# A decoder's first self-attention: the bias band added by TensorE, side work at later tiles, larger gathers, and value jobs of the cross-attentions at other key tiles

## The reference, cut to what matters

```python
# first self-attention: 16 heads of 16, on _layernorm(x)
rel = pos[:, None] - pos[None, :]                       # query minus key
bias = jnp.minimum(rel * slopes[:, None, None], 8.0)    # slopes[h] = 2 ** (-(h + 1) / 2)
scores = einsum('bhqd,bhkd->bhqk', q, k) * D ** -0.5 + bias
x = x + softmax(scores) @ v @ out_proj_weight.T + out_proj_bias
# cross-attention: 8 heads (masked, layer 0) or 16 heads (layer 1) of 64
x = x + (softmax(q @ k.T * 64 ** -0.5) @ v) @ W_o + b_o
```

## Time and profile before

| what | us |
|---|---|
| median of 3 runs (3207.7 to 3210.42) | 3209.64 |
| the profiled execution's own time | 3209.26 |
| its span, first to last instruction | 3207.5 |
| first self-attention, stage start to first score tile | 117.5 to 172.2 |
| its loop, first to last exponential | 173.3 to 509.1 |
| first cross-attention, exponentials | 572.4 to 1317.3 |
| second cross-attention, exponentials | 1564.4 to 3055.0 |

### The profile page before, as it was taken

How to read it: one execution, slowest core, us unless ns; L and a number is a source line. 1 busy time by engine, 2 the same in 40 slices (tenths; PEclk the granted TensorE clock), 3 DMA queues, 4 the chain that set the end, 5 groups by cost and what they waited for, 6 DMA issues and landing times. The chain is left out here.

```text
span 3207.5 us, 38273 instructions
## 1 busy us (share of the span) xinstructions
PE 2823.4 (88%) x12634; PEld 1744.4 (54%) x12634; DVE 1851.7 (58%) x3753; ACT 1302.5 (41%) x2326; POOL 1648.4 (51%) x1404
## 2 busy tenths in 40 slices
PE   6578786899999999688899999999999999999979
PEld 5333344556565565354655655565556556566457
DVE  2356675566666666536555655555565565565556
ACT  1134554444444454311444444444444444444410
POOL 0344402566566666610466665666666666666710
PEclk8778998999999999898899999999999999999979
DMA  8666513232232322100332232232322233222110
GB/s 266 157 167 151 142 15 90 54 99 67 63 89 64 90 58 56 35 0 22 102 73 49 64 101 49 68 73 58 90 66 67 55 99 75 49 67 63 31 53 27
DMA packets 113532, 245.81 MB, mean 77 GB/s; under 512 B 15366, under 2 KB 61703, under 8 KB 112184
## 3 DMA queue, kind: packets, MB, share of 16 engines
q1 hardware_dynamic: 107128, 219.82, 27.6%
q0 software_dynamic: 5696, 23.42, 2.7%
q10 hardware_dynamic: 512, 0.13, 0.0%
HBM read 107.31 MB, written 31.76 MB: 43 GB/s over the span
## 5 line engine op out<-in xcount | busy, mean ns | idle before, releaser
L1009 POOL TENSOR_TENSOR ACC<-ACC,PR 128x512 f32<-128x512 f32 (+1 forms) x1056 | 1331.1, 1283 | 486.2 <-ACT PR L1234 476.8
L1234 ACT ACTIVATE PR<-banks 128x512 f32<-128x512 f32 (+1 forms) x832 | 469.1, 597 | 682.6 <-PE banks L1123 681.2
L1295 DVE TENSOR_REDUCE mx<-banks 128x2 f32<-128x800 f32 (+1 forms) x512 | 504.2, 986 | 406.8 <-PE banks L1075 405.6
L1139 PE MATMUL banks<-PR,V 128*64 128x512 f32 (+1 forms) x2496 | 602.5, 607 | 0.0
L1122 PE MATMUL banks<-QA,KA 128*128 128x512 f32 (+1 forms) x1248 | 535.4, 429 | 9.7 <-DMA QB<-ROW 8.7
L1075 PE MATMUL banks<-KH,QZ 128*128 128x400 f32 (+1 forms) x1536 | 482.7, 372 | 58.2 <-DVE mx L1295 37.9
L1123 PE MATMUL banks<-QB,KB 65*128 65x512 f32 (+1 forms) x1248 | 495.0, 397 | 0.0
L1075 PEld LDWEIGHTS banks<-KH,QZ 128*128 128x128 f32 x1536 | 268.3, 189 | 246.5 <-issue 113.6
L1234 ACT ACTIVATE PR<-banks,small 128x512 f32<-128x512 f32 (+1 forms) x416 | 269.3, 687 | 306.5 <-PE banks L1123 298.8
L1292 DVE CUSTOM_DVE_ANT_0 banks<-banks,maskadd 128x400 f32<-128x400 f32 (+1 forms) x512 | 289.9, 588 | 158.5 <-PE banks L1075 153.0
L1263 DVE TENSOR_TENSOR KB<-banks,KH 64x400 fp32r<-64x400 f32 (+1 forms) x384 | 219.4, 571 | 261.4 <-ACT KH L1167 255.9
(11 more groups left out here) (240 smaller groups left out, 3047.0 us busy)
## 6 DMA issues: line engine op xcount, KB each, us to landing
KA<-KH SPq DMA_DIRECT2D x192, 400.5 KB, 6.7
CX<-ctx_split SPq DMA_DIRECT2D x8, 2403.0 KB, 10.7
WK<-wk_split SPq DMA_DIRECT2D x48, 256.0 KB, 5.7
WV<-wv_split SPq DMA_DIRECT2D x24, 512.0 KB, 3.6
QA<-QZ SPq DMA_DIRECT2D x96, 128.0 KB, 2.3
QB<-QZ SPq DMA_DIRECT2D x96, 128.0 KB, 2.4
first<-in_w_in SPq DMA_DIRECT2D x8, 1024.0 KB, 6.0
second<-in_w_out1T SPq DMA_DIRECT2D x8, 1024.0 KB, 8.7
```

Source lines behind the costliest of these rows:

```text
L1009: pool.tensor_tensor(acc, other, PR[0:r, n % RING, :], ALU.add).then_inc(summed, 1)
L1139: last = pe.matmul(OB[h * DH:(h + 1) * DH, :], V[0:r, g % 4, s, h * DH:(h + 1) * DH], PR[0:r, (n + h) % RING, :], start=(s == 0), stop=(s ...
L1234: act.activation(PR[0:r, n % RING, :], SB[n % 3][0:r, :], ACT.Exp, bias=keybias[0:r, g // pairs, t:t + 1] if masked else 0.0).then_inc(pro ...
L1295: dve.tensor_reduce(mx[:, :, t, c], couples[i % 2 if g == 0 else 0][:, :, 0:w], AX.X, ALU.max).then_inc(mx_done, 1)
```

## The change

- **Band.** TensorE adds it: after the score matmul of a banded tile a second one, fp32, with minus the identity (`minus`, 128 x 128) as weights and the band (128 partitions by up to 128 columns) as moving side accumulates into the same bank. VectorE's subtraction and the semaphore `biased` are gone.
- **Side work.** `LEAD` is 24. The jobs stand at other tiles (p 0, 4, 20, 29; v 45, 48; a 13, 16; o 32, 36; turn 7, row 10, of a batch or a group). ScalarE does a job one tile later than TensorE and HI two tiles later; VectorE does LO four tiles later, v and o two later, and `normalise` at tile 9.
- **Gathers.** `parts` holds three blocks per side, so SyncE stores high twice (HI as soon as it is there), 48 stores of 256 KB in place of 32, and gathers with four DMAs per half of 48 partitions by 8 KB, q before k, 32 DMAs in place of 96. The weights are permuted on the host so that a partition's four rows are adjacent.
- **Start.** TensorE runs `before()` ahead of the wait for the rows, with the two "v" between the second and third "p". GpSimd starts to split only when the first row has landed.
- **Cross-attentions.** Three "v" jobs stand at t 5, 7, 9, four at 4, 5, 7, 9. Mask steps stand at t 11 (step 0), 12 (1 and 2) and 13 (3).

```diff
--- before.py
+++ after.py
@@ -89,7 +89,7 @@
-        self.parts = nc.dram_tensor("parts", (2, 2, 4, P, S), F32).ap()
+        self.parts = nc.dram_tensor("parts", (2, 4, 2, 3, DH, S), F32).ap()
...
@@ -401,10 +401,10 @@
-        LEAD, RING = 22, 8
+        LEAD, RING = 24, 8
...
-        HALF = 12 * 16
+        HALF = 4 * 16
...
@@ -416,25 +416,21 @@
-            return [("p", 0, i) for i in range(4)] + [("v", 0, 0), ("v", 0, 1)]
+            return [("p", 0, 0), ("p", 0, 1), ("v", 0, 0), ("v", 0, 1), ("p", 0, 2), ("p", 0, 3)]
...
-                jobs += {1: [("p", b + 1, 0)], 3: [("p", b + 1, 1)], 17: [("p", b + 1, 2)], 19: [("p", b + 1, 3)],
-                         34: [("v", b + 1, 0)], 37: [("v", b + 1, 1)]}.get(l, [])
+                jobs += {0: [("p", b + 1, 0)], 4: [("p", b + 1, 1)], 20: [("p", b + 1, 2)], 29: [("p", b + 1, 3)],
+                         45: [("v", b + 1, 0)], 48: [("v", b + 1, 1)]}.get(l, [])
...
-                jobs += {13: [("a", b - 1, 0)], 15: [("a", b - 1, 1)], 25: [("o", b - 1, 0)], 29: [("o", b - 1, 1)]}.get(l, [])
-            if n % GN == 6 and n >= GN:
+                jobs += {13: [("a", b - 1, 0)], 16: [("a", b - 1, 1)], 32: [("o", b - 1, 0)], 36: [("o", b - 1, 1)]}.get(l, [])
+            if n % GN == 7 and n >= GN:
...
-            if n % GN == 11 and n // GN + 1 < NG:
+            if n % GN == 10 and n // GN + 1 < NG:
...
@@ -460,6 +456,7 @@
+            minus = sb("minus", [P, P])
...
@@ -491,24 +488,24 @@
-                            for side in range(2):
+                            for side, kinds in ((0, "hlh"), (1, "hhl")):
...
-                                c = 2 * side + half
-                                sp.wait_ge(lo_ready, i + 1)
+                                to = self.parts[b % 2, 2 * side + half]
...
-                                sp.dma_start(self.parts[b % 2, 0, c], raw(HI[:, i % 2, :])).then_inc(hl_out[i % 2], 16)
-                                sp.dma_start(self.parts[b % 2, 1, c], raw(LO[:, i % 2, :])).then_inc(hl_out[i % 2], 16)
-                            for side in range(2):
-                                sp.wait_ge(hl_out[side], 32 * (2 * b + half + 1))
+                                sp.wait_ge(hi_ready, i + 1)
+                                for blk in range(3):
+                                    if kinds[blk] == "h":
+                                        sp.dma_start(to[:, blk], raw(HI[:, i % 2, :])).then_inc(hl_out[i % 2], 16)
+                                sp.wait_ge(lo_ready, i + 1)
+                                sp.dma_start(to[:, kinds.index("l")], raw(LO[:, i % 2, :])).then_inc(hl_out[i % 2], 16)
...
-                            for side, to, parts in ((1, KS, (0, 0, 1)), (0, QS, (0, 1, 0))):
-                                for blk, part in enumerate(parts):
-                                    src = self.parts[b % 2, part, 2 * side + half].rearrange("(i two d) n -> two d i n", two=2, d=D)
-                                    for par in range(2):
-                                        o = DH * par + D * blk
-                                        sp.dma_start(raw(to[o:o + D, b % 2, 4 * half:4 * half + 4, :]), src[par]).then_inc(stacked[half], 16)
+                            for side, to in ((0, QS), (1, KS)):
+                                sp.wait_ge(hl_out[side], 48 * (2 * b + half + 1))
+                                for par in range(2):
+                                    src = self.parts[b % 2, 2 * side + half, par].rearrange("k (d i) n -> (k d) i n", d=D)
+                                    sp.dma_start(raw(to[DH * par:DH * par + 48, b % 2, 4 * half:4 * half + 4, :]), src).then_inc(stacked[half], 16)
...
@@ -519,6 +516,7 @@
+                    pool.wait_ge(row_in, 32)
...
@@ -601,10 +599,11 @@
+                    for x in before():
+                        job(x)
+                    pe.wait_ge(scaled, 1)
...
-                    for x in before():
-                        job(x)
...
@@ -614,8 +613,13 @@
-                        pe.matmul(SB[n % 3][:, :], operand(KS, h, ROWS)[:, t * P:(t + 1) * P], operand(QS, h, ROWS),
-                                  start=True, stop=True).then_inc(sc_ready, 1)
+                        last = pe.matmul(SB[n % 3][:, :], operand(KS, h, ROWS)[:, t * P:(t + 1) * P], operand(QS, h, ROWS),
+                                         start=True, stop=not banded(n))
+                        if banded(n):
+                            o = t * P + int(CLAMP[h % H])
+                            w = min(P, S - o)
+                            last = pe.matmul(SB[n % 3][:, o:o + w], minus[:, :], self.band[:, h % H, 0:w], start=False, stop=True)
+                        last.then_inc(sc_ready, 1)
...
@@ -636,11 +640,9 @@
-                                act.wait_ge(hl_out[j % 2], 32 * (j // 2))
+                                act.wait_ge(hl_out[j % 2], 48 * (j // 2))
...
-                            act.wait_ge(job_done, i + 1)
-                            act.activation(HI[:, j % 2, :], FULL[:, j % 2, :], ACT.Copy).then_inc(hi_ready, 1)
...
@@ -655,26 +657,33 @@
+                    def rounded(x):
+                        j = 4 * x[1] + x[2]
+                        act.wait_ge(job_done, place[x] + 1)
+                        act.activation(HI[:, j % 2, :], FULL[:, j % 2, :], ACT.Copy).then_inc(hi_ready, 1)
+
...
-                    act.wait_ge(scaled, 2)
+                    act.wait_ge(scaled, 3)
...
+                        if x[0] == "p":
+                            rounded(x)
...
-                        if banded(n):
-                            act.wait_ge(biased, bands[n + 1])
-                        else:
-                            act.wait_ge(sc_ready, n + 1)
+                        act.wait_ge(sc_ready, n + 1)
...
-                        for x in at(n):
+                        for x in at(n - 2) if n >= 2 else []:
+                            if x[0] == "p":
+                                rounded(x)
+                        for x in at(n - 1) if n >= 1 else []:
...
@@ -730,6 +739,7 @@
+                    dve.tensor_scalar(minus[:, :], ident[:, :], -1.0, None, ALU.mult).then_inc(scaled, 1)
...
@@ -738,17 +748,15 @@
-                        if banded(n):
-                            o = t * P + int(CLAMP[h % H])
-                            w = min(P, S - o)
-                            dve.wait_ge(sc_ready, n + 1)
-                            s = SB[n % 3][:, o:o + w]
-                            dve.tensor_tensor(s, s, self.band[:, h % H, 0:w], ALU.subtract).then_inc(biased, 1)
-                        for x in at(n):
-                            job(x)
...
-                        if n % GN == 7 and g >= 1:
+                        for x in at(n - 4) if n >= 4 else []:
+                            if x[0] == "p":
+                                job(x)
+                        for x in at(n - 2) if n >= 2 else []:
+                            if x[0] in "vo":
+                                job(x)
+                        if n % GN == 9 and g >= 1:
...
@@ -813,8 +821,10 @@
-            if t >= 4:
-                jobs += values_at(g)[t - 4:t - 3]
+            todo = values_at(g)
+            for x, tile in zip(todo, {0: (), 3: (5, 7, 9), 4: (4, 5, 7, 9), 7: range(4, 11)}[len(todo)]):
+                if tile == t:
+                    jobs.append(x)
...
@@ -1376,8 +1386,9 @@
-                            if masked and g % pairs == 1 and g // pairs + 1 < B and t in (0, 11, 12, 13):
-                                mask_step(g // pairs + 1, (0, 11, 12, 13).index(t))
+                            if masked and g % pairs == 1 and g // pairs + 1 < B:
+                                for c in {11: (0,), 12: (1, 2), 13: (3,)}.get(t, ()):
+                                    mask_step(g // pairs + 1, c)
...
@@ -1852,14 +1863,20 @@
+    def paired(w):
+
+        w = w.copy()
+        w[..., 0:2 * C] = w[..., 0:2 * C].reshape(-1, 4, H // 4, 2, D).transpose(0, 1, 3, 4, 2).reshape(w[..., 0:2 * C].shape)
+        return w
+
...
-        "w0_in": g["L0_attn_in_proj_weight"].T, "b0_in": g["L0_attn_in_proj_bias"],
-        "b0_cols": g["L0_attn_in_proj_bias"][0:2 * C].reshape(4, P).T,
+        "w0_in": paired(g["L0_attn_in_proj_weight"].T), "b0_in": g["L0_attn_in_proj_bias"],
+        "b0_cols": paired(g["L0_attn_in_proj_bias"])[0:2 * C].reshape(4, P).T,
```

More of the change, by code:

```diff
@@ L417, in banded @@
             return S - 1 - t * P > CLAMP[h % H]
-        bands = [0]
-        for n in range(N):
-            bands.append(bands[-1] + banded(n))
         def before():
-            return [("p", 0, i) for i in range(4)] + [("v", 0, 0), ("v", 0, 1)]
+            return [("p", 0, 0), ("p", 0, 1), ("v", 0, 0), ("v", 0, 1), ("p", 0, 2), ("p", 0, 3)]
         def at(n):
@@ L476, in self_attention @@
                 scaled, ones_made, x_based = sem("s_scaled"), sem("s_ones"), sem("s_based")
-                sc_ready, biased, probs, used, mx_ready, mx_done = (
```

(5 more changed lines are left out.)

## The result

The changed kernel takes **3286.5 us** (median of 4 runs, 3275.6 to 3289.8) against 3208.7 of the kernel before: ratio 1.0243, 95% interval 1.0218 to 1.0269. That is 78 us slower where 62 us faster was forecast, and outside the range. The profiled execution took 3285.4 us, its span is 3283.6.

What follows compares the result with a forecast made beforehand. No engine fills the self-attention loop, a ring of short waits; TensorE bounds the cross-attentions, though not every tile. Start -12, loop -21, mask steps -14 and value jobs -15 sum to -62 against 3209.3: 3147 us, range 3110 to 3188.

Steps and rivals of the forecast that it cites:

- The loop: Self-attention loop, 335.8 us before: sum of opposite terms for projections, band, turn, normalise and row's DMA, -21 us.
- Normalise at 9 with row at 10: Self-attention loop: TensorE stands at row behind normalise, 1.5 us in each of 15 groups, +23, ends 0 and +30.
- Band on TensorE: Self-attention loop: 0.35 us per band, 53 us of TensorE, half hidden in its 61 idle us, +27, ends +0 and +75.
- Rival C: Banded loop groups: TensorE becomes the bound through the second matmul, kernel slower by 20 us, 3229; chance 0.04.
- the drain at a change of tiling mode: Banded loop tiles: two mode changes each might drain TensorE; neither proved nor excluded, counted as Rival C's mechanism.
- Projections: Loop groups with "p" jobs: LO four tiles later removes 85% of VectorE's 32.7 us wait for HI, -28.
- Turn one tile later: Self-attention loop: removes about half of TensorE's 25.6 us wait for the copied outputs before "turn", -13.
- The start: Before the loop: earlier first copy, and q gathers sent sooner in fewer, larger DMAs, -12 us.
- SyncE's queue issues 64 fewer gathers and 16 more stores and was idle anyway: The start: the changed counts of gathers and stores on SyncE's queue were taken to cost nothing.
- GpSimd's last piece: GpSimd's splitting starts later; its last piece moves from 385.7 to about 415 to 425, at no cost.
- Mask steps and value jobs: Cross-attentions: later mask steps give -14 us, value jobs moved to odd key tiles give -15 us.

Runs made afterwards that it cites:

- g1: f7 with the next tile's score repeated six times, as overwritten matmuls, before each row job: 3180.0 us.
- f7: f3 with turn, normalise and row moved to tiles 7, 9 and 10, and the two o jobs at 28 and 31: 3223.0 us.
- h1: The whole changed kernel with split stores, plus six overwritten score matmuls before each row job: 3219.5 us.
- e3: The changed kernel with each store issued as two DMAs of 64 partitions (split stores): 3261.5 us.
- g5: f3 with row at tile 10 in place of 11, normalise still at 7, and LEAD 24 in place of 22: 3170.1 us.
- e1: The kernel before with only the band moved to TensorE: 3207.4 us, ratio 1.0010.
- g2: f7 with the band back on VectorE: 3177.9 us.
- h4: g5 with the band back on VectorE: 3175.3 us.
- h3: The whole changed kernel with split stores and the band back on VectorE: 3206.3 us.
- f6: The changed kernel with split stores, ScalarE and VectorE doing each job's result in the tile that issues it (no lags): 3240.0 us.
- e4: The kernel before with only the cross-attention parts, the moved mask steps and value jobs: 3176.4 us, ratio 0.9901.
- f3: The changed kernel with split stores, but the self-attention's side work, lags and LEAD 22 as in the kernel before: 3174.8 us.

## Why the prediction was wrong

- **The loop, -21 forecast, +93 measured. The step that failed is "Normalise at 9 with row at 10", +23 with ends of 0 and +30.** Its mechanism and its own size were right: TensorE stands at row 13 times, 19.4 us in all. What it left out is what an idle TensorE does next: its clock falls to 1.2 GHz, and that is worth 43 us (g1 against f7) and 42 us (h1 against e3) in a kernel whose TensorE has no slack. Both ways of keeping TensorE at work there won it back: throwaway matmuls in the wait (g1, 3180.0), and `normalise` three tiles ahead (g5, 3170.1).
- **"Band on TensorE", +27, ends 0 and +75.** At 2.4 GHz it was about right: a banded tile passes in 0.84 us (299.00 to 299.84 in f7), of which 0.41 lies between the band's start and the next pair (299.43 to 299.84), 62 us for 152 bands where 53 was taken, and e1 shows them hidden. At 1.2 GHz the same takes 1.44 and 0.72 us (539.57 to 541.01 and 540.29 to 541.01 in the changed kernel). I counted TensorE's idle 61 us as cover and took the clock as given; but it is not given, the other term of the same sum sets it. The two terms were added up, though each makes the other dearer: the band alone 0 (e1), turn, normalise and row alone about 0 (g2), both together 48 us (f7).
- **Rival C, 0.04**, had the right engine and nearly the right price of a band (0.81 us at 1.2 GHz, 0.72 measured), though its +20 in all is far below the +78, and was held down by the clocks of groups in which, before, no wait stood at tile 10. No run shows the drain at a change of tiling mode, of which the Trainium skill, "TensorEngine Tiling (Array Packing)", Key Properties, speaks, by itself: whatever the two changes in a banded tile cost is within the 0.41 us, and in e1 it was hidden.
- **"Projections", -28, and "Turn one tile later", -13**: no such gain shows. In the loop of the changed kernel VectorE hardly waits at LO any more, and "turn" no longer waits for the copied outputs (24.7 us in h4, nothing in g2), but the time went elsewhere: g2 is 3 us above h4, and h3, with the other tiles and the lags, 28 us above g2. Its waits name the jobs' lags: "turn" for FULL (10.4 us in h3) and X (7.1). The new tiles and the lags were not told apart beyond f6, which is 21 us faster without the lags; what the tiles and LEAD cost each stays open.
- **The start, -12 forecast, +13 measured** (stage start to first exponential). "SyncE's queue issues 64 fewer gathers and 16 more stores and was idle anyway" is the failed step: it counted stores by number and took one to be as cheap as before; one took 5 us. With stores split (e3) the first maximum comes at 142.8, where 142 was forecast, and the stretch takes 45.4 us against 55.8: 10 of the forecast 12. GpSimd's last piece was issued at 466.6 us, not near 420; the stage ended long after it, so it cost nothing.
- **Mask steps and value jobs, -29**: right (the first cross-attention's value jobs come to 2.1, not 2.4, by the prices that stand there). Tile 2 of pair 1 takes 6.01 us, as written; the traces give -34, and e4 gives 32 with the interval 23 to 40.

The ladder, with medians: 3208.7 less 32 (cross parts) is 3176; start, gathers and band, nothing (f3, 3174.8); turn, normalise, row and the shifted "o" jobs +48 (f7); the other tiles, the lags and LEAD +38 (e3), of which only the lags were tried by themselves (f6); slow stores +25: 3286.

## What to carry to other kernels

Before TensorE gets more work, ask what the clock will be: when TensorE is the bound, waits of 1 to 2 us at one job in its queue can cost more than twice their own length (18.9 us of them, 48 us in f7), since everything behind them may run at 1.2 GHz. Keep a producer on another engine several tiles ahead of the job that waits for it, and test a suspicion by filling the wait with throwaway matmuls: if the kernel gets faster, it was the clock. Look at a new store's slowest dimension before calling its issue free.

## What the runs showed of the hardware

- Once low, the clock can stay low under full load. The changed kernel's group at 537.43 was busy 34.5 of 35.1 us at 0.50, and over the whole low stretch, 522.6 to 573.8, it was idle for 0.7 us; what ends such a stretch stays open. The Trainium skill, "TensorE: Matmul & The Clock Gate", Part 1, ties the clock to how busy TensorE has been; the falls behind the row wait agree, this stretch doesn't by itself.
- More work on TensorE can raise its clock: moving the band onto it cut the loop's low time from 84 to 9 us (e1), and from 94 to 19 (h4 to g5). It is no rule: with a wait at row left in, the same move raised it from 130 to 171 us (g2 to f7).
- A 256 KB store took 0.3 to 0.5 us of its queue with a target whose slowest dimension was 128, and 3.9 to 5.0 us, behind others of its kind, with one of 2.
